# Seven half-size products for eight in the experts' first matmul of a two-layer kernel, with new instruction orders

## What is computed

```python
def _L1_ffn_ref(x, gate_w, w1, w2):          # 8 experts, d = 256, hidden f = 1024
    k = int(EXPERT_CAPACITY * t / e)          # 128 tokens per expert and batch
    probs = jax.nn.softmax(jnp.einsum('ntd,ed->nte', x, gate_w), axis=-1)
    g, m = jax.lax.top_k(probs.transpose(0, 2, 1), k)
    xin = x[batch_idx, m]
    h = jnp.einsum('nekd,edf->nekf', xin, w1)
    h = jax.nn.gelu(h, approximate=False)
    h = jnp.einsum('nekf,efd->nekd', h, w2)
    out = jnp.zeros((n, t, d)).at[batch_idx, m].add(g[..., None] * h)
```

## Time and profile before

| | |
|---|---|
| median of 3 runs | 1941.64 us (1941.33 to 1943.31) |
| span of the profiled execution | 1941.7 us |
| TensorE busy | 1911.9 us, 98% |
| VectorE, ScalarE, GpSimd busy | 1093.9, 919.0, 694.8 us |
| chain that ended last | TensorE 96%, VectorE 2%, ScalarE 1% |
| L982 (hidden) | 1024 records, 234.3 us busy |
| L995 (output) | 1024 records, 226.7 us busy |

### The profile page before, as it was taken

One profiled execution on the slowest core, in us unless ns is written; L12 is line 12 of the kernel. 1 busy time (PEld: TensorE's weight loads), 2 busy tenths in 40 slices (PEclk: granted clock), 3 DMA queues, 4 the chain that ended last, 5 costly groups with the idle time before them and its releaser, 6 DMA issues.

```text
span 1941.7 us, 30308 instructions
## 1 busy us (share of the span) xinstructions
PE 1911.9 (98%) x11192; PEld 1317.8 (68%) x11192; DVE 1093.9 (56%) x2904; ACT 919.0 (47%) x1970; POOL 694.8 (36%) x769
## 2 busy tenths in 40 slices
PE   8989999999999999999999999999999999999998
PEld 5835655765575666557656655665786888888887
DVE  5767676558556746656585655577534447223221
ACT  5646666556565555655665566454334321111111
POOL 3302334334332433252343324343443433333332
PEclk9989999999999999999999999999999999999999
DMA  3020001000000100010001000050130223333333
GB/s 129 2 87 15 12 1 39 1 23 12 28 23 1 39 1 23 1 39 15 9 13 28 13 10 15 23 176 2 31 85 4 59 73 98 66 76 79 85 76 70
DMA packets 59696, 76.78 MB, mean 40 GB/s; under 512 B 7120, under 2 KB 52824, under 8 KB 59296
## 3 DMA queue, kind: packets, MB, share of 16 engines
q1 hardware_dynamic: 46448, 57.28, 8.9%
q0 software_dynamic: 12288, 16.79, 5.0%
q10 hardware_dynamic: 816, 0.79, 0.1%
HBM read 53.71 MB, written 21.00 MB: 38 GB/s over the span
## 4 chain that ended last, share of the span: by engine, by line
PE 96%; DVE 2%; ACT 1%; DMA 0%; issue 0%; POOL 0%; SPq 0%; ACTq 0%; DVEq 0%; POOLq 0%
PE bank L765 15%; PE bank L982 12%; PE bank L995 11%; PE bank L832 7%; PE bank L887 4%; PE bank L856 4%; PE bank L868 4%; PE bank L781 3%; PE bank L750 3%; PE bank L591 3%; PE bank L900 3%; PE bank L617 3%; PE bank L841 3%; PE bank L712 2%; PE bank L818 2%; PE bank L692 2%
## 5 line engine op out<-in xcount | busy, mean ns | idle before, releaser
L1232 ACT ACTIVATE h<-bank 128x512 f32<-128x512 f32 x128 | 76.3, 597 | 363.9 <-PE bank L982 352.8
L982 PE MATMUL bank<-xin,ew 128*128 128x256 f32 x1024 | 234.3, 381 | 0.0
L995 PE MATMUL bank<-ew,h 128*128 128x256 f32 x1024 | 226.7, 379 | 0.0
L1776 POOL TENSOR_TENSOR s<-s,ri 128x256 f32<-128x256 f32 (+3 forms) x128 | 160.0, 1268 | 156.5 <-DVE ri L1531 156.5
L995 PEld LDWEIGHTS bank<-ew,h 128*128 128x128 f32 x1024 | 194.2, 190 | 27.7 <-issue 1.5
L982 PEld LDWEIGHTS bank<-xin,ew 128*128 128x128 f32 x1024 | 189.5, 190 | 23.4 <-issue 0.2
L1814 POOL DMA_INDIRECT out<-y,indices x64 | 104.2, 1628 | 265.9 <-DVE y L1668 164.9
L1208 ACT ACTIVATE s<-s,mn 128x128 f32<-128x128 f32 (+3 forms) x256 | 141.0, 552 | 109.0 <-DVE mn L1524 108.9
L1509 DVE SCALAR_TENSOR_TENSOR th<-th,bank 128x384 f32<-128x384 f32 (+1 forms) x192 | 104.3, 594 | 112.0 <-ACT th L1199 110.6
L1668 DVE SCALAR_TENSOR_TENSOR y<-bank,gates,gbe 128x256 f32<-128x256 f32 x64 | 31.0, 484 | 238.5 <-PE bank L995 230.1
L832 PE MATMUL bank<-look,term 128*128 128x384 f32 (+3 forms) x512 | 152.7, 438 | 0.0
(11 more groups left out here) (320 smaller groups left out, 3641.3 us busy)
## 6 DMA issues: line engine op xcount, KB each, us to landing
ew<-L_ffn_w SPq DMA_DIRECT2D x24, 1024.0 KB
x1s<-x_scratch SPq DMA_DIRECT2D x8, 512.0 KB
out<-x1s SPq DMA_DIRECT2D x8, 512.0 KB, 2.9
xn_scratch<-n_xn SPq DMA_DIRECT2D x8, 512.0 KB, 2.9
x<-L_attn_x SPq DMA_DIRECT2D x7, 512.0 KB, 3.8
x_scratch<-x SPq DMA_DIRECT2D x7, 512.0 KB, 3.0
wqkv<-w_qkv SPq DMA_DIRECT2D x1, 3072.0 KB, 10.7
wqkv<-L_wmod SPq DMA_DIRECT2D x2, 1024.0 KB, 8.0
```

Of the source, the lines that this page charges most:

```text
L982: mm = te.matmul(banks[i][:, g * 2 * P:(g + 1) * 2 * P], w1[:, kk, (2 * n + g) * P:(2 * n + g + 1) * P], xin[:, kk, :, :].rearrange("p h s ...
L995: mm = te.matmul(banks[i][:, 0:D], ex.h1[:, g, n * P:(n + 1) * P], w2[:, g, :], start=(g == 0), stop=(g == FC - 1))
L1776: done = g.tensor_tensor(sc, sc, b1.ri[u % 2][:, m, :].unsqueeze(2).to_broadcast([P, 2, w]), ALU.mult)
```

## The change

For the 28 units of loads 0 to 7 the four `hidden` steps become four `seven` steps; the last four units keep `hidden`. The product of w1 (two halves of d by two halves of the 1024 features) with xin (two halves of d by two batches) is made as seven products of 512 features by 128 tokens, each over one half of d, in place of eight. Each is four matmuls of 128 columns. Four of the seven are added up one after another in a single PSUM bank, the chain: between two of them the bank is read in its present state, first by ScalarE (`first_read`), then twice by VectorE (`chain_read`); the other three fill banks of their own. VectorE adds these to the parts of `h1`, and ScalarE then takes the gelu of three quarters of `h1` in place and of the last from the bank. VectorE also makes four sums of `xin` halves per unit (`mix_x`, 128x128), and GpSimd four sums of w1 quarters per load (`mix_w`, 128x512), one of them in place in w1. `output` takes the batches in the other order. NBUF falls from 3 to 2. The three tables are written anew.

```diff
-NBUF = 3
+NBUF = 2
+def new_load(m):
+    return seven(m) and UNITS[m][2] != UNITS[m - 1][2]
...
+    if seven(m):
+        yield "seven", m, 0
+        if m + 3 < NUNIT:
+            yield "pick", m + 3, 0
+        yield "seven", m, 1
+        yield "seven", m, 2
+        if m + 1 < NUNIT:
+            yield "turn_x", m + 1, 0
+        yield "seven", m, 3
...
+            if n == 0:
+                te.wait_ge(k.weights_in[load % NBUF], 32 * (load // NBUF + 1))
...
+                chained(w1[:, 0, 0:F // 2], xin[:, 0, 0, :], True).then_inc(s["chain"], 1)
+            elif n == 1:
+                te.wait_ge(s["mixed_w"], 4 * (load + 1))
+                te.wait_ge(s["mixed_x"], 4 * (b + 1))
+                te.wait_ge(drained[i5], n5 - 1)
+                product(i5, sums[:, 0, :], xt[:, 0, :]).then_inc(full[i5], 1)
+                te.wait_ge(s["first_read"], b + 1)
+                chained(sums[:, 1, :], xt[:, 1, :], False).then_inc(s["chain"], 1)
+            elif n == 2:
+                te.wait_ge(drained[i3], n3 - 1)
+                product(i3, sums[:, 2, :], xin[:, 1, 1, :]).then_inc(full[i3], 1)
+                te.wait_ge(s["chain_read"], 2 * b + 1)
+                chained(w1[:, 0, F // 2:F], xt[:, 2, :], False).then_inc(s["chain"], 1)
+                te.wait_ge(drained[i2], n2 - 1)
+                product(i2, w1[:, 1, 0:F // 2], xin[:, 1, 0, :]).then_inc(full[i2], 1)
+            else:
+                te.wait_ge(s["chain_read"], 2 * b + 2)
+                chained(w1[:, 1, F // 2:F], xt[:, 3, :], False).then_inc(full[i1], 1)
...
+            if n == 1:
+                v.wait_ge(s["chain"], 3 * b + 2)
+                v.wait_ge(drained[i5], n5)
+                v.tensor_tensor(ex.h1[:, tops, P:2 * P], chain, ex.h1[:, lows, P:2 * P], ALU.add
+                                ).then_inc(s["chain_read"], 1)
+            elif n == 2:
+                v.wait_ge(full[i3], n3)
+                v.wait_ge(s["chain_read"], 2 * b + 1)
+                v.tensor_tensor(ex.h1[:, tops, P:2 * P], ex.h1[:, tops, P:2 * P], third, ALU.add).then_inc(drained[i3], 1)
+                v.wait_ge(s["chain"], 3 * b + 3)
+                v.tensor_tensor(ex.h1[:, lows, P:2 * P], chain, ex.h1[:, lows, P:2 * P], ALU.add
+                                ).then_inc(s["chain_read"], 1)
...
+        elif step == "mix_w" or step == "seven" and n == 0 and new_load(b + 1):
+            load = b if step == "mix_w" else UNITS[b + 1][2]
...
+            g.wait_ge(k.weights_in[load % NBUF], 32 * (load // NBUF + 1))
+            g.tensor_tensor(sums[:, 0, :], w1[:, 0, low], w1[:, 1, low], ALU.add).then_inc(mixed, 1)
```

Of the tables, the start of HEAD:

```diff
-    0stats:0 0silu:0 1stats:0 0wqkv_load:0 0mod_load:0 0x0:0 0norm:0 1norm:0 0cols:0 0setup:0 1x0:0 0mod_load:1
-    0w0_load:0 0cols:1 0feat:0 0rows:0 1feat:0 0kq:0 1mod_load:0 0kq:1 1mod_load:1 0v:0 0bias0:0 0setup0:0
+    0silu:0 0stats:0 1stats:0 0mod_load:1 0w0_load:0 0cols:0 0norm:0 0wqkv_load:0 1norm:0 0x0:0 0cols:1 0feat:0
+    0mod_load:0 1x0:0 1feat:0 0setup:0 0rows:0 0kq:0 0kq:1 0v:0 1mod_load:1 0setup0:0 1silu:0 0sc0:0 0sc0:1 0wt0:0
```

284 lines of the change are left out of this document (184 added, 100 removed).

## The result

The changed kernel takes 1957.83 us (median of 4 runs, 1956.32 to 1961.08), before 1941.55; the ratio is 1.0085, with a 95% interval of 1.0071 to 1.0099. It is slower by 16 us, where I forecast 1935.6 with a range of 1924 to 1951.

What follows compares the result with a forecast made beforehand. The prediction took TensorE's records in a row to bound the kernel, the other engines having room. Its terms summed as 1941.7 - 20.7 + 4.8 + 1.8 + 1 + 11.0 - 4 = 1935.6 us, range 1924 to 1951.

Steps and rivals of the forecast that it cites:

- term 6: New order elsewhere in the tables: fewer changes between whole and part array on TensorE, -4 us; the rest +-4.
- Term 1: Expert units: 56 records of 128 columns at 0.110 us replace 32 of 256, -20.7 us over 28 units.
- The time of some 2010: Alternative kernel time in us, if 128-column records cost 0.16 us each by the skill page's ratio of 1.5.
- Term 2: Waits inside the chain: 0.17 us a unit, +4.8 over 28 units, plus +1.8 for the second choice.
- The part on the second choice: Units where a `top` stands between VectorE's chain reads: 0.6 us more in each of three units, +1.8.
- `pick` is in time by a microsecond: `pick`, ahead of VectorE's read of link 1, is done a microsecond before that link's last record and costs 0.
- Terms 3 and 4: Sums on VectorE and GpSimd cost +1 us (0 to +9), GpSimd being idle 63%; two weight buffers cost 0.
- Term 5: Kernel start: `w0_load` DMAs stand ahead, TensorE's first product at 20.5 in place of 9.00 us, +11.0.
- rival C: The start shifts less, later HEAD work having waited for other engines anyway; the 11 us are absorbed, 1925; chance 0.08.
- B: Links among attention's steps wait behind other ScalarE and VectorE work, +21 us, 1957; chance 0.14.
- A: Weight loads are not hidden under 128 columns in the expert units: 125 us more, 2060; chance 0.03.
- D: Orders laid out worse or better than could be seen: either side of 1941.7 by 8 us; chance 0.08.

Runs made afterwards that it cites:

- best3: Changed kernel with early start, PERIOD of before, 7norm:1 ahead of 5sc:2 in LAST, index and fetch between second and third seven steps in units 12 to 27: 1945.0 us.
- best2: Changed kernel with early start, PERIOD of before, two items moved in LAST, and GpSimd's weight sums issued a unit earlier: 1955.4 us.
- eight_new_tables: Changed kernel's three tables and two buffers, but eight products for all 32 units and no sums of x and w: 1969.5 us.
- start_early: Changed kernel with cT, the 512-column part of wmod and inputs x0 and x1s issued ahead of w0_load again in HEAD: 1949.6 us.
- all_old_blocks: All three tables of before with the seven products, LAST changed only so that a unit's four seven steps stand in a row: 1977.7 us.

## Why the prediction was wrong

The step that failed is term 6: it put the waits of a new order at nothing, and they cost about 16 us.

**Term 1 (seven for eight)** held. Its price of 0.110 a record was 0.1115, so that 56 cost 6.24 and not 6.16: 2.3 us in 28 units. Rows 4 had that number, 0.111, as the distance of weight loads; whether the loads or the 128 columns set the pace no run here shows. The sustained distance that the Trainium skill gives for 128 columns (page "TensorE: Matmul & The Clock Gate", section "Back-to-back issue gap") does not show here. The time of some 2010 that the prediction worked out from it adds up to 2014 with its own terms.

**Term 2 (the chain)** held in its main part: link 1's reader is VectorE's, and what it was to cost, 0.14 + 0.04 a unit, is 0.16 + 0.05. What it consists of I had wrong: not TensorE's restart of 0.14, but 0.06 of wait and second records that come 0.10 and 0.05 late. best3's 13.93 shows that 0.21 us of cover take away all of the 0.16. The part on the second choice was too small: 1.8 for 4.4. Its 0.6 for the second read was 0.49, three times, as forecast. Its step "`pick` is in time by a microsecond" failed where tops stand ahead of `pick`, which I had looked at only in a unit without them, and the wait of 1.4 for the ranks at the end had no term.

**Terms 3 and 4 (sums, buffers)** came out near nothing in the changed kernel: no wait of TensorE for the sums or weights. But the reason I gave, GpSimd's idle time, was not the one that matters. The sums stop VectorE, which costs nothing only as long as `output` covers it; best2 and best3 are what it costs elsewhere.

Terms 1 to 4 together were to give 13.1 us, and eight_new_tables against the changed kernel gives 11.7. That it comes so near is luck: with the lost clocks of eight_new_tables taken off it is 8.5, and the units add up to the same, 28 times 0.66 for term 1 less 28 times 0.20 for the chain and some 4.6 for the second choice, or 8.2.

**Term 5 (the start)** was 11.0 and is 8.2 by start_early. The first product came at 19.1 for 20.5; 2 to 3 us of it are absorbed, so rival C is true to a fifth or a quarter.

**Term 6 (the order elsewhere)** is where the prediction failed: -4, with an unknown of 4 either way, for what is 27.3 - 8.2 = 19.1 by eight_new_tables, and 16.4 in the changed kernel, which did not lose the clock (1957.8 = 1941.6 - 8.4 + 8.2 + 16.4). Both halves of it failed. The changes between whole and part arrays, which I counted (they went from 169 to 153), were to save 3.0 to 4.5, 0.6 to 0.8 of it in each period; net of waits a period takes 175.5 us in both tables, so they saved nothing that shows. And the waits had no term: "of the rest, rows show nothing: +-4". In a period of before TensorE waited in one place, at a cost of 0.33 us, so there was nothing to win and much to lose. They come to 2.1 us in each of the first three plays of PERIOD and to 5.8 in LAST, with 1.7 for each clock that is lost behind one.

**Rivals.** B, links that wait behind attention's work, did not happen in the changed kernel: between 1410 and 1600 us no link waits over 0.1 us, and of the first seven distances between outputs six are shorter than with eight products (0.45 to 0.6 us, and one 3.0 with a lost clock on the other side in it) and one 0.4 longer. It did happen in all_old_blocks. A did not. D named the right part, the order, with a chance of 0.08 and half of the size. My range ended at 1951 because an order was allowed to cost 8.

## What to carry to other kernels

When a change comes with a new order, price the order by itself: play the old work in the new order first, since a schedule tuned to within tenths of a microsecond of its bound has far more to lose than to gain, and rows of the old trace can't show the new waits. A wait that was filled by moving one item mostly moved on here, to the next product that needs the same engines. Before GpSimd gets work "for free", look for what VectorE does on SBUF at the same time, and keep its short operations ahead of a chain out of that overlap.
